# Mixture-of-experts tail on one core: slot numbers computed before the shared rows' first products, expert rows loaded two pairs ahead, two PSUM banks for the pairs' sums

## What is computed

```
logits = x @ w_router.T                 # 16 experts, TOP_K = 1
mask   = one_hot(top_k(logits)); scores = sigmoid(logits) * mask
gate, up = split(einsum('eth,ehf->etf', scores.T[:, :, None] * x, gate_up_proj))
expert_out = einsum('etf,efh->eth', up * silu(gate), down_proj)
shared = silu(x @ w_gate.T) * (x @ w_up.T) @ w_down.T
out    = x_in + shared + expert_out.sum(axis=0)
```

## Time and profile before

| | us |
|---|---|
| median of 3 runs (lowest to highest) | 642.89 (642.54 to 643.53) |
| the profiled execution | 641.85 |
| its span, first to last instruction | 639.7 |
| PE busy, with 1809 instructions | 522.9 (82%) |
| DVE busy, with 799 instructions | 493.5 (77%) |
| POOL busy, with 394 instructions | 382.3 (60%) |
| ACT busy, with 530 instructions | 252.4 (39%) |

### The profile page before, as it was taken

One profiled execution on the slowest core, in us unless ns is written; L12 is line 12 of the kernel. 1 busy time (PEld: TensorE's weight loads), 2 busy tenths in 40 slices (PEclk: granted clock), 3 DMA queues, 4 the chain that ended last, 5 costly groups with the idle time before them and its releaser, 6 DMA issues.

```text
span 639.7 us, 7393 instructions
## 1 busy us (share of the span) xinstructions
PE 522.9 (82%) x1809; PEld 273.2 (43%) x1810; DVE 493.5 (77%) x799; ACT 252.4 (39%) x530; POOL 382.3 (60%) x394
## 2 busy tenths in 40 slices
PE   3889898989999886966786789889999967766883
PEld 2543434444444333322454455434544255434551
DVE  5697999989898999799899998688999773413331
ACT  4476543444444332110533344525455115121341
POOL 2378776757576465654776233476676575674553
PEclk9999999999999998898999799989999975976997
DMA  6801137900000691000521123200000011123440
GB/s 171 202 19 33 33 85 215 232 1 1 1 1 1 165 341 53 2 0 0 153 70 49 35 83 90 50 17 25 25 25 17 1 50 41 37 79 93 116 105 9
DMA packets 49572, 43.57 MB, mean 68 GB/s; under 512 B 5160, under 2 KB 42790, under 8 KB 49160
## 3 DMA queue, kind: packets, MB, share of 16 engines
q1 hardware_dynamic: 45220, 36.67, 21.6%
q0 software_dynamic: 3280, 6.09, 3.4%
q10 hardware_dynamic: 1040, 0.43, 0.2%
HBM read 24.80 MB, written 19.37 MB: 69 GB/s over the span
## 4 chain that ended last, share of the span: by engine, by line
PE 34%; DVE 31%; issue 16%; POOL 13%; ACT 3%; DMA 2%; SPq 1%; POOLq 0%; DVEq 0%; ACTq 0%
DVE grown L1531 10%; PE ps L1999 8%; PE ps L2016 5%; POOL grown L1131 5%; DVE ps L1565 4%; PE ps L1952 3%; DVE early L1637 3%; PE ps L2006 2%; PE ps L2056 2%; POOL uv L1045 2%; DVE early L1632 2%; DVE grown L1553 2%; PE ps L1757 2%; POOL slot_rows L1060 2%; PE ps L2057 2%
## 5 line engine op out<-in xcount | busy, mean ns | idle before, releaser
L1131 POOL TENSOR_TENSOR grown<-grown 128x512 f32<-128x512 f32 x64 | 80.5, 1268 | 91.7 <-DVE grown L1553 91.7
L1531 DVE TENSOR_TENSOR grown<-ps,steps 128x1536 f32<-128x1536 f32 x64 | 112.2, 1753 | 1.6
L1952 PE MATMUL ps<-grown,cst 128*128 128x512 f32 x128 | 72.8, 652 | 24.6 <-DVE grown L1531 24.2
L926 ACT ACTIVATE uv<-ps 128x512 f32<-128x512 f32 x64 | 38.1, 597 | 104.8 <-DVE grown L1553 104.8
L1999 PE MATMUL ps<-steps 128*128 x128 | 70.1, 646 | 8.2 <-issue 8.2
L1045 POOL TENSOR_TENSOR uv<-uv,steps 128x512 f32<-128x512 f32 x64 | 67.5, 1076 | 1.6 <-ACT uv L926 1.6
L1953 PE MATMUL ps<-grown,cst 128*128 128x512 f32 x128 | 68.0, 614 | 0.0
L1962 PE MATMUL ps<-uv,cst 128*128 128x512 f32 x128 | 60.4, 594 | 1.1 <-POOL uv L1045 1.1
L1423 DVE TENSOR_TENSOR e_h<-rk,ps 128x256 f32<-128x256 f32 x64 | 25.2, 417 | 42.7 <-ACT rk L943 29.4
L1207 POOL TENSOR_TENSOR early<-state,qT 128x512 f32 x22 | 37.1, 1688 | 34.0 <-DVE state L1545 34.0
L1553 DVE TENSOR_TENSOR grown<-ps,steps 128x512 f32<-128x512 f32 x64 | 43.3, 677 | 7.6 <-PE ps L1952 7.6
(11 more groups left out here) (233 smaller groups left out, 1022.8 us busy)
## 6 DMA issues: line engine op xcount, KB each, us to landing
steps<-gate_up_proj SPq DMA_DIRECT2D x1, 4096.0 KB, 16.1
xs_others<-zeros SPq DMA_DIRECT2D x1, 2496.0 KB, 10.8
steps<-xs_others SPq DMA_DIRECT2D x19, 128.0 KB, 2.1
ys_others<-e_y SPq DMA_DIRECT2D x19, 128.0 KB, 1.8
early<-chain_m SPq DMA_DIRECT2D x4, 512.0 KB, 6.2
xf<-x SPq DMA_DIRECT2D x4, 495.0 KB
normed<-early SPq DMA_DIRECT2D x28, 64.0 KB, 1.7
slot_rows<-no_row SPq DMA_DIRECT2D x1, 1741.5 KB, 13.9
```

Source lines behind the costliest of these rows:

```text
L1131: G.tensor_tensor(decayed[:, h], decayed[:, h], work[:, h, 1], ALU.add).then_inc(s_add[h], 1)
L1531: V.tensor_tensor(grown[:, :, h].rearrange("p e (x w) -> p e x w", w=HD), st, per_col(tile, FF, 3, h, HD), ALU.mult).then_inc(s_prod[h], 1)
L1952: T.matmul(bank[2 * h + 1], c["block"], work[:, h, 1], start=True, stop=True).then_inc(s_usum[h], 1)
```

## The change

It has four parts.

1. In `route`, the two first products of the shared rows are done after the slot numbers are out (L1393), ahead of the tiles' experts (L1396), no longer between L1382 and L1386.
2. SP loads the rows of pair 3 ahead of its wait for the base scatters, and then in step k the rows of pair k+2, where it was k+1. The waits of each load on `s_et` and `s_to` stay as they were.
3. The sums of pair k of RUNS[2] go to bank 2 or 3 in turn, and `down(k)` waits for `add_base(k-2)`, where it was `add_base(k-1)`. For the other rows' runs nothing changes.
4. The stores of the other rows, and the wait for `s_fin` ahead of them, begin in step 3, where it was step 2. There are still 20, two in a step.

```diff
         def b_y(run):
-            return bank[6][:, U * P:] if run is RUNS[1] else bank[2][:, 0:U * P]
+        def b_y(run, b):
+            return bank[6][:, U * P:] if run is RUNS[1] else bank[2 + (b if run is RUNS[2] else 0)][:, 0:U * P]
...
-            for k in range(3):
+            for k in range(4):
                 load_rows(k)
             sp.wait_ge(s_based, 16 * MIXED.n)
             for k in range(2):
                 load_base(k)
             for k in range(2, run.n):
-                if k + 1 < run.n:
-                    load_rows(k + 1)
+                if k + 2 < run.n:
+                    load_rows(k + 2)
                 load_base(k)
-                if k == 2:
+                if k == 3:
                     sp.wait_ge(s_fin, 2)
-                for b, part in stores[2 * k - 4:2 * k - 2]:
-                    store_others(b, part)
+                if k >= 3:
+                    for b, part in stores[2 * k - 6:2 * k - 4]:
+                        store_others(b, part)
...
                 link(V.tensor_tensor(r_ts, r_ti, r_nt, ALU.subtract))
-                if m:
-                    shared_h(t, 0, 0)
-                    shared_h(t, 0, 1)
                 link(V.tensor_tensor(r_inc, r_inc, r_tot, ALU.subtract))
...
                 V.tensor_tensor(q["idx"][:], q["slot"], c["spare_" + t.name], ALU.add).then_inc(s_idx, 1)
+                if m:
+                    shared_h(t, 0, 0)
+                    shared_h(t, 0, 1)
...
             def down(run, i, k, of):
-                pe.wait_ge(s_eo, i + (k + run.g0 + 1))
+                pe.wait_ge(s_eo, i + (k + run.g0 + (0 if run is RUNS[2] and (type(i) is not int or i + k) else 1)))
...
-                        ins = T.matmul(b_y(run)[:, u * D:(u + 1) * D], e_hT[:, u, f * P:(f + 1) * P],
+                        ins = T.matmul(b_y(run, k % 2)[:, u * D:(u + 1) * D], e_hT[:, u, f * P:(f + 1) * P],
```

More of the change, by code:

```diff
@@ L399, in b_gu @@
             return (bank[0], bank[1]) if b and run is not RUNS[1] else (bank[4], bank[5])
-        def b_y(run):
-            return bank[6][:, U * P:] if run is RUNS[1] else bank[2][:, 0:U * P]
+        def b_y(run, b):
+            return bank[6][:, U * P:] if run is RUNS[1] else bank[2 + (b if run is RUNS[2] else 0)][:, 0:U * P]
         b_gate, b_up, b_tok = (bank[0], bank[2]), (bank[1], bank[3]), bank[7]
@@ L951, in copy_y @@
                 act.wait_ge(s_ew[b], written)
-                S.activation(e_y[:, b], b_y(run).rearrange("p (u d) -> p u d", u=U), ACT.Copy).then_inc(s_eo, 1)
+                S.activation(e_y[:, b], b_y(run, b).rearrange("p (u d) -> p u d", u=U), ACT.Copy).then_inc(s_eo, 1)
             def pairs(run):
@@ L1708, in add_base @@
                     dve.wait_ge(s_ew[b], 16 * (1 + run.base[b]))
-                V.tensor_tensor(e_y[:, b], b_y(run).rearrange("p (u d) -> p u d", u=U), e_base[:, b], ALU.add
+                V.tensor_tensor(e_y[:, b], b_y(run, b).rearrange("p (u d) -> p u d", u=U), e_base[:, b], ALU.add
                                 ).then_inc(s_eo, 1)
```

## The result

The changed kernel takes 633.18 us (median of 4 runs, 630.86 to 633.35). On the same occasions the kernel before took 642.71 (median of 4, 640.96 to 643.53). The ratio is 0.9847, 95% interval 0.9816 to 0.9878: about 9.5 us less. The forecast was 634.4, with a range of its own of 633.4 to 635.6, which the median leaves by 0.2 us, and a full one of 631.8 to 638.8.

The account below looks back on a forecast made before the run. Waits along the tail's chain (slot numbers, base rows, pair rows) bound it, then PE. 6.45 us up to `h_transposes(2)` (4.15 and 2.3), then 7.78 for 9.87 us, sum 8.5: 642.89 - 8.5 = 634.4 us, range 631.8 to 638.8.

Parts of the forecast that it names:

- Its own signs: Trace signs in the tail: pairs 3 and 4 waits under 0.5 us, `add_base(0)` about 34.5 us after L1382, 4.10 per pair.
- Part 1, 4.15 us: Slot numbers out 4.15 us earlier; POOL's whole scatter string moves with them, gaining 4.15 us up to the base rows.
- Part 2, rows ahead: PE's waits for rows of pair 3 (4.37 us) and pair 4 (2.09 us) go, through earlier SP loads.
- Part 3, two banks: `down(1)` and pair 3's first gate-and-up product run during the base-row wait; at 0 in full flow.
- The rival in which `down(1)` is still held: Bases still hold `down(1)` and pair 4 is late: 4.15 us gained, 638.7; chance 0.17 shared by three cases.
- What is late next: PE's `h_transposes(2)` wait for `gate(2)` behind `add_base(0)` and a large addition; 6.45 us gained up to there.
- The clock: PE from `h_transposes(2)` to pair 3's down products: 7.78 us at low clock, 5.35 at full clock, which gives 10.9 gained.
- Part 4, cost 0: Stores a pair later, the last two hidden under the last output scatters; cost 0, otherwise the time of two stores.
- The rule against it: DVE's large addition blocks POOL's second output scatter, pair 5's rows at about 582.2: 0 at low clock, 0.3 us at full.
- Full clock: Rival: PE stays at 2.4 GHz ahead of `h_transposes(2)`; gain 10.9 less up to 0.7 us, 632.0 to 632.7; chance 0.2.
- The stall at pair 5: Rival: row load behind POOL's token copy stalls pair 4 or 5; 4.24 us gained, 638.7; chance 0.17 for three cases.
- The stall in every step: Rival: rows of pair k+2 wait for `tokens(k)` in SP's queue, 4.26 us each; 647.2 with three; chance 0.04.

Follow-up runs that it names:

- c_after: The changed kernel unaltered, measured a second time; 632.70 us, ratio 0.9868 to the kernel before.
- after: The changed kernel against the kernel before, first measurement with its profiled execution; 633.18 us, ratio 0.9847.
- e1: The kernel before with only the two shared products moved behind the slot numbers; 637.24 us, ratio 0.9949 to the kernel before.
- e3: The changed kernel with one bank for the sums of all pairs, `down(k)` waiting for `add_base(k-1)` again; 632.95 us, ratio 0.9878.
- e4: The changed kernel with pair 3's rows loaded behind the first two base loads again; 633.34 us, ratio 0.9870.
- e9: The changed kernel with pair 3's rows loaded only when POOL has issued its last base scatter; 630.44 us, ratio 0.9848.
- e2: The changed kernel with the two shared products put back ahead of the slot numbers; 636.28 us, ratio 0.9928.
- e8: e7 with both large additions ahead of `add_base(0)` and pair 3's token copy ahead of the first output scatter; 627.37 us, ratio 0.9792.
- e10: e5 with one bank for the sums of all pairs, `down(k)` waiting for `add_base(k-1)`; 632.70 us, ratio 0.9882.
- e7: Changed kernel with `gate(2)` and the first large addition ahead of `add_base(0)`, pair 4's rows loaded ahead of SP's base-scatter wait; 631.02 us, ratio 0.9834.
- e6: The changed kernel with both large additions ahead of `gate(0)`, amid POOL's string of scatters; 629.59 us, ratio 0.9820.
- e5: The changed kernel with both large additions ahead of `add_base(0)`, once POOL has issued its last base scatter; 629.62 us, ratio 0.9825.

## Why the prediction was right

The sum was right to 0.2 us in the first profile (8.68 measured up to `down(3)`, 8.54 worked out), with errors inside it that cancel. In the second (c_after) the gain to `down(3)` was 10.41, and the other end that I gave was 10.9.

- **The median.** 633.18 was measured for 634.4. Of these 1.2 us, 1.04 are the step from the profiled execution to the median, which I took over from the kernel before. In the changed kernel the two agree (633.17 and 633.18). The range of its own was missed by 0.2 us for this reason.
- **Its own signs.** Two signs of being right failed, PE's wait for pair 3 under 0.5 us (1.83, in c_after 1.20) and `add_base(0)` about 34.5 us after `r_ts` (35.82 and 34.99). One of the signs of being wrong came: `add_base(0)` moved by 2.82 and 3.65 us, not by 4. The total holds in spite of them; the next points say why.
- **Part 1, 4.15 us.** Right where it was worked out: slot numbers after 2.38 us, POOL's start 4.15 earlier against `r_ts` (3.17 for 7.32 us), the string unchanged at 26.85. What failed is the sentence that "all of it moves by 4.15", for two reasons. The landing of the last scatter is not POOL's pace: it took 1.26 us more in after and 0.60 in c_after. And where it was on time (e1, e3, e4, e9: 3.8 to 3.9 us gained), the string was 0.3 to 0.4 us longer, by the operation on the tiles' experts that now runs beside it; I had looked at when that result is needed, not at what it does to POOL. The cover for the later shared rows held: against `r_ts` the last shared addition came 0.36 us later (forecast 0.3), and nobody waited for it.
- **Part 2, rows ahead.** I said pair 3's rows would land 2.1 to 3.0 us after issue and PE would wait under 0.5. They took 4.55 us (issue 568.66, PE at 573.21) and PE waited 1.83. In e2 and e8 there was no wait. Pair 4's wait is gone as said. The miss cost little, because PE would have waited for DVE all the same.
- **Part 3, two banks.** `down(1)` runs ahead of `add_base(0)`, as said. That part 2 "would gain nothing there" without it was too strong: with one bank (e3) `h_transposes(2)` come 4.16 us after `add_base(0)`, 4.75 with part 1 alone (e1) and 2.47 with all parts. The rival in which `down(1)` is still held had 638.7 only with pair 4 late as well; e3 has the one without the other, and takes 632.95. "Cost 0 in flow" was the wrong side of zero: C is 35.29 to 35.54 in the four profiles with one bank (before, e1, e3, e10) and 34.85 to 35.09 in the nine with two, a gain of about 0.4 us over nine pairs that I did not price.
- **What is late next.** Right: `h_transposes(2)` behind `add_base(0)` and the addition, 2.47 us after it, forecast 2.8.
- **The clock.** I took 7.78 us from there to `down(3)`, the value that two waits of 4.37 and 2.09 us had left behind, and gave 5.35 as the full-clock end. Measured: 6.63 with the low clock (after) and 5.73 without (c_after). The low stretch, where it came, was shorter than the term I put in; it followed 1.83 and 1.91 us of idle time with work between, not "some 3 us" in one. Mis-sized by 1.15 us, this term made up for the late landing, and that was luck. Of the 0.38 us by which 5.73 passes 5.35, some tenths are pair 5's rows: PE's transposes of them start 0.08 us after the products ahead end, where they otherwise start 0.15 before.
- **Part 4, cost 0.** Right: no row of the changed kernel waits for a store, and its last stores end under the scatters.
- **The rule against it.** Each scatter that began beside an addition ended 0.87 or 0.88 us after that addition: 578.78 for 577.90 and 581.17 for 580.30 here, 577.27 for 576.39 in e1. A scatter alone takes 0.97 to 1.00. So the second scatter took 2.08 us, not the 1.3 of POOL's pace, and the trace sides with the Trainium skill (SBUF — State Buffer, Who interferes with whom), by which the one that issues second is blocked. In the trace the scatter that began second ended 0.87 us after the addition, which is nearly its whole time alone. The other order is not as in that rule: where a scatter began first, DVE's product of two SBUF inputs was not held (0.57 us in after). It cost nothing at the low clock and some tenths at the full one, as worked out. In e7, where PE was earlier, 0.86 us of PE's wait would be its doing (a scatter of 1.86 for 1.00), by my reckoning; no run moves the second addition alone.
- **The rivals.** Full clock (632.0 to 632.7) had 0.2. It is half of the truth: one of the two profiled executions of the changed kernel ran so, and the medians, 633.18 and 632.70, lie between its upper end and the forecast. How many runs go which way isn't known, since only profiled ones show the clock of a stretch. The stall at pair 5 did not come with this change and came with e7. The stall in every step had no sign: POOL's pace in the flow is 1.28 us a scatter, and C did not grow.

## What to carry to other kernels

When a chain of dependent small operations releases a long string on another engine, put nothing between its links: here two products of 0.69 us, with their waits, held the string back by 4.15 us, of which e1 shows 3.9 at the pairs' start. After removing such a wait, look at what the same engine still does ahead of the next consumer; here the two large additions held another 1.7 us, with up to 0.95 of low clock behind it, and hid what the second bank was worth: undoing the bank did not show in the time until they were moved. Price a transfer that ends a chain by its spread, not by one landing. And look at where the part begins that you changed: two kernels here had low medians and a tail no shorter than the changed kernel's.

## What the runs showed of the hardware

- An indirect DMA issued by POOL that begins while an addition of DVE with both inputs in SBUF runs is held until the addition ends: base scatters of 0.97 us became 1.83 and 1.10 in e6, output scatters 1.65 and 2.08 in after; without an addition beside them 1.00 and 0.99 in e5. POOL's cast is held as well (1.48 us for 0.20 in e1). Where the scatter began first, neither was seen to be held: in after, e7, e8 and e10 the scatter took 0.98 us and DVE's product of two SBUF inputs 0.57.
- From the last base scatter's start to the first base load took 2.25 to 3.52 us in different profiled executions, and a row load beside it was used 2.17 (e3) to 4.55 us (after) from its issue. The cause is open.
- The same program had its clock at 0.51 for 3 us behind waits of 1.83 and 1.91 us in one execution, and at 1.00 throughout behind 1.20 and 1.76 us in another. Across the kernels the length of the waits does not tell either: 0.50 behind 1.16 and 1.40 us in e6, 1.00 behind 1.04 and 2.19 in e7.
